# A fused perceiver layer on one core: the order of TensorE's work over the 64 tiles of cross-attention, taken two tiles at a time

## The reference, cut to what matters

```python
x = x + xattn(layernorm(x), ctx)      # x (2,128,128), ctx (2,2048,128), 16 heads of 8
x = x + attn(layernorm(x))            # self-attention over 128 rows, rotary and ALiBi
x = x + ffn(layernorm(x))             # 16 experts of 512, top 4, gelu

# xattn, the part that the change is about
scores = einsum('bhqd,bhkd->bhqk', Qh, Kh) / sqrt(8)
scores = scores - max(scores, axis=-1)
attn = softmax(scores); attn = clip(attn, 1e-12); attn = attn / sum(attn)
ctx = einsum('bhqk,bhkd->bhqd', attn, Vh)
```

## Time and profile before

| | |
|---|---|
| median of 3 runs | 209.88 us (209.35 to 210.08) |
| the profiled execution | 209.72 us, its span 207.8 us |
| TensorE matmul busy | 190.0 us (91%), 2552 instructions |
| VectorE busy | 144.4 us (69%), of it 75.2 us in 64 reductions (L609) |
| ScalarE busy | 143.9 us (69%), of it 69.4 us in 128 exponentials (L1025) |
| GpSimd busy | 82.4 us (40%) |
| granted TensorE clock | 1.00 of full speed from 34 to 128 us |
| tiles | scores of tile 0 start at 34.71 us, those of tile 34 at 81.27, of tile 52 at 107.66 |
| time outside the tiles | the experts run from about 129.7 us to the end |

### The profile page before, as it was taken

The page is one execution under the profiler, slowest core; times in us unless marked ns, Lnnn a source line. Parts: engine busy times, 40 slices in busy tenths (PEclk is TensorE's granted clock), DMA queues, the critical chain, the costliest instruction groups (busy, mean ns, idle before and its releaser), DMA issues.

```text
span 207.8 us, 6327 instructions
## 1 busy us (share of the span) xinstructions
PE 190.0 (91%) x2552; PEld 134.1 (65%) x2552; DVE 144.4 (69%) x259; ACT 143.9 (69%) x321; POOL 82.4 (40%) x117
## 2 busy tenths in 40 slices
PE   4799988999999989989999999999879999999991
PEld 1335235656666545655655666897759998999981
DVE  5289998797979978989999945856884438222220
ACT  4768766888897978876797976778574545456660
POOL 6222979997786987110201001510000005078400
PEclk9999999999999999999999999999999999999999
DMA  5834333366334732367868701400000000000000
GB/s 122 295 140 183 145 93 93 99 221 226 93 93 105 203 106 78 98 209 214 278 222 250 244 19 24 185 0 0 5 0 0 3 0 13 3 0 5 0 0 21
DMA packets 8688, 21.24 MB, mean 102 GB/s; under 512 B 1664, under 2 KB 2784, under 8 KB 8656
## 3 DMA queue, kind: packets, MB, share of 16 engines
q1 hardware_dynamic: 7344, 19.47, 29.3%
q0 software_dynamic: 592, 0.74, 1.6%
q10 hardware_dynamic: 720, 0.59, 0.9%
HBM read 17.52 MB, written 3.28 MB: 100 GB/s over the span
## 4 chain that ended last, share of the span: by engine, by line
PE 61%; DVE 15%; POOL 7%; DMA 6%; issue 4%; ACT 3%; SPq 2%; ACTq 1%; DVEq 0%
PE ps L1516 13%; PE ps L1266 11%; PE ps L1549 10%; PE ps L1247 8%; PE ps L1212 5%; PE ps L1122 3%; DMA wks<-in_wk 3%; DVE sm L712 2%; PE ps L1116 2%; SPq L327 2%; DMA parts_d<-w1s 2%; POOL wr L505 1%; DVE kst L710 1%; DMA kst<-parts_d 1%; PE ps L1409 1%
## 5 line engine op out<-in xcount | busy, mean ns | idle before, releaser
L609 DVE TENSOR_REDUCE mx<-ps 128x2 f32<-128x1024 f32 x64 | 75.2, 1221 | 7.6 <-PE ps L1212 7.5
L1025 ACT ACTIVATE ex<-ps 128x512 f32<-128x512 f32 x128 | 69.4, 594 | 15.0 <-PE ps L1247 12.1
L1266 PE MATMUL ps<-ex,vau 128*9 128x128 f32 x1024 | 39.9, 274 | 0.5 <-ACT oS L1040 0.4
L1516 PE MATMUL ps<-xT,w1s 128*128 128x128 f32 x256 | 34.4, 278 | 0.2
L1516 PEld LDWEIGHTS ps<-xT,w1s 128*128 128x128 f32 x256 | 31.1, 192 | 1.7 <-ACT cT L1051 0.8
L1247 PE MATMUL ps<-qst,kst 64*128 64x128 bf16 x512 | 30.2, 217 | 1.5 <-ACT ex L1025 1.1
L807 DVE SCALAR_TENSOR_TENSOR xs<-ps,wr,xs 128x128 f32<-128x128 f32 x32 | 11.2, 350 | 28.6 <-PE ps L1549 28.3
L1266 PEld LDWEIGHTS ps<-ex,vau 128*9 128x9 f32 x1024 | 22.0, 90 | 13.7 <-ACT ex L1025 9.7
L1247 PEld LDWEIGHTS ps<-qst,kst 64*128 64x128 bf16 x512 | 18.5, 94 | 16.9 <-ACT ex L1025 9.1
L1212 PE MATMUL ps<-kst,qst 64*128 64x512 bf16 x128 | 27.2, 382 | 1.7 <-DMA kst<-parts_d 0.8
L1051 ACT ACTIVATE cT<-ps,b1s 128x128 f32<-128x128 f32 x64 | 18.2, 370 | 13.8 <-PE ps L1516 13.8
(11 more groups left out here) (205 smaller groups left out, 250.4 us busy)
## 6 DMA issues: line engine op xcount, KB each, us to landing
kst<-parts_d SPq DMA_DIRECT2D x84, 64.0 KB
w1s<-in_w SPq DMA_DIRECT2D x8, 512.0 KB, 4.2
kst<-in_w SPq DMA_DIRECT2D x8, 512.0 KB, 4.5
parts_d<-w1s SPq DMA_DIRECT2D x4, 768.0 KB, 3.8
cT<-in_ctxT SPq DMA_DIRECT2D x3, 512.0 KB, 5.0
cT<-in_ctxT SPq DMA_DIRECT2D x2, 256.0 KB, 5.0
picks<-in_pick ACTq DMA_DIRECT2D x1, 384.0 KB, 5.4
qkvs<-in_qkvw POOLq DMA_DIRECT2D x1, 192.0 KB, 3.6
```

Of the source, the lines that this page charges most:

```text
L609: dve.tensor_reduce(out=mx2[:, b, 2 * pair:2 * pair + 2, f], in_=ps[:, bank:bank + 2, :], axis=AX.X, op=ALU.max).then_inc(s["redA"], 1)
L1025: act.activation(ex[:, e % NE, :], ps[:, EBANK["exp", e], :], ACT.Exp, scale=SCALE).then_inc(s["exp"], 1)
L1266: last = pe.matmul(ps[32 * j:32 * j + DK + 1, 7, 128 * hg:128 * hg + 128], vau[:, NK * b + c, GH * hg + j, :], ex[:, (2 * t + j % 2) % NE, ...
L1516: last = pe.matmul(ps[:, SELF[j % 2], 128 * n:128 * n + 128], w1s[:, f0:f0 + 128], xT[:, (b % B) * S:(b % B + 1) * S], start=True, stop=True)
```

## The change

Tiles with units are issued in twos, an even tile `t` and `t + 1`: 25 pairs, from 0 to 51, but for tiles 32 and 33, which stay single, as do those from 52 on. In a pair TensorE does `scores(t)`, a unit, half 0 of `scores(t + 1)`, a unit, half 1, and then `values(t - 1)` and `values(t)` in one run. If `t` has a ring job, that job and the second unit stand between the two tiles, and `scores(t + 1)` is whole. For that all ring jobs have even tiles now: the value pieces move from 3, 11, 19 to 4, 12, 20, and the projection, normalised rows, qkv and q/k turn by one tile. There are 6 exponential buffers, and the exponential of tile `t` waits for `values(t - 3)` where it waited for `values(t - 2)`. The two new buffers hold `picks` and `qr` before the first tile, so ScalarE waits once for GpSimd's last use of `qr`.

```diff
-        picks = sb("picks", [128, 2, 2, 3, 128], bf16)
...
-        qr = sb("qr", [128, B * S])
...
-        NE = 4
+        NE = 6
         ex = sb("ex", [128, NE, 512])
+        early = ex[:, 4:NE, :].rearrange("p a k -> p (a k)")
+        picks = early[:, 0:768].bitcast(bf16).rearrange("p (q h t m) -> p q h t m", q=2, h=2, t=3)
+        qr = early[:, 768:768 + B * S]
...
-        SMALL_AT = {34: "sums", 36: "heads", 39: "proj", 41: "normed", 43: "qkv", 47: "qkT"}
-        VALS_AT = {3: 5, 11: 6, 19: 7}
+        SMALL_AT = {34: "sums", 36: "heads", 40: "proj", 42: "normed", 44: "qkv", 48: "qkT"}
+        VALS_AT = {4: 5, 12: 6, 20: 7}
...
+        def paired(t):
+            return t // 2 != TILES // 4 and t + 8 + LEAD < N_UNITS
...
-                if u == 51:
+                if u == 52:
                     normed(1, [0])
...
-                if t >= 2:
-                    act.wait_ge(s["pv"], t - 1)
+                if t >= NE // 2:
+                    act.wait_ge(s["pv"], t - NE // 2 + 1)
...
+            act.wait_ge(s["qsq"], 1)
...
+            def two_tiles(t):
+
+                scores(t)
+                next_unit(t)
+                if ring_job(t):
+                    job(t)
+                    next_unit(t + 1)
+                    scores(t + 1)
+                else:
+                    scores(t + 1, (0,))
+                    next_unit(t + 1)
+                    scores(t + 1, (1,))
                 if t:
                     values(t - 1)
+                values(t)
+
+            def one_tile(t):
+
+                scores(t)
+                job(t)
+                next_unit(t)
+                self_first(t)
+                values(t - 1)
+
+            for t in range(0, TILES, 2):
+                if paired(t):
+                    two_tiles(t)
+                else:
+                    one_tile(t)
+                    one_tile(t + 1)
```

More of the change, by code:

```diff
@@ L456, in _ @@
             pool.wait_ge(s["qparts"], 1)
-            link(pool.tensor_tensor(qf[:], qr[:], qp[:, 0, :], ALU.add))
+            link(pool.tensor_tensor(qf[:], qr, qp[:, 0, :], ALU.add))
             pool.tensor_tensor(qsq[:], qf[:], qf[:], ALU.mult).then_inc(s["qsq"], 1)
@@ L580, in q_parts @@
                 dve.wait_ge(s["q0"], 1)
-                link(dve.scalar_tensor_tensor(out=qr[:], in0=ps[:, 7, B * S:2 * B * S], scalar=cols[:, 0:1], in1=qp[:, 0, :],
+                link(dve.scalar_tensor_tensor(out=qr, in0=ps[:, 7, B * S:2 * B * S], scalar=cols[:, 0:1], in1=qp[:, 0, :],
                                               op0=ALU.add, op1=ALU.subtract))
-                link(dve.tensor_copy(qp[:, 1, :], qr[:]))
-                dve.tensor_tensor(qp[:, 2, :], qr[:], qp[:, 1, :], ALU.subtract).then_inc(s["qparts"], 1)
+                link(dve.tensor_copy(qp[:, 1, :], qr))
+                dve.tensor_tensor(qp[:, 2, :], qr, qp[:, 1, :], ALU.subtract).then_inc(s["qparts"], 1)
             def norms_max(bank):
@@ L930, in _ @@
             act.dma_start(wqs[:], wq).then_inc(d_wq, 16)
-            act.dma_start(picks[:].rearrange("p q h t m -> p (q h t m)").bitcast(i32), pick_in).then_inc(d_pick, 16)
+            act.dma_start(early[:, 0:768].bitcast(i32), pick_in).then_inc(d_pick, 16)
             act.wait_ge(s["pool"], 1)
@@ L1481, in next_unit, with job @@
                     unit(t + 8 + LEAD)
[L1483 to L1489, removed]
+            def job(t):
                 if turns(t):
@@ L1496, in _ @@
                     vals(VALS_AT[t], EBANK["vals", VALS_AT[t]])
-                if not ring_job(t - 1):
-                    next_unit(t)
-                self_first(t)
+            def two_tiles(t):
[9 more added lines that the diff above has]
+                    scores(t + 1, (1,))
                 if t:
                     values(t - 1)
+                values(t)
[11 more added lines that the diff above has]
+                    one_tile(t + 1)
             values(TILES - 1)
```

## The result

Over 20 runs the changed kernel takes 210.39 us in the median, the kernel before 209.55 us in as many. The ratio is 1.0041, with a 95% interval of 1.0027 to 1.0054: slower by 0.6 to 1.1 us. The forecast was 210.7 us against 209.88, a ratio of 1.004. In some executions of every kernel here the time is some 3 us longer; the medians count them and the ratios leave them out, and the two of which the profile was kept, of e4 and e12, differ from the others by a tile 0 that starts some 3 us late.

The account below looks back on a forecast made before the run. A ring of three score banks between TensorE and ScalarE bounds the tiles. Tiles 0 to 31 give -0.2 us and 34 to 51 +1.1: +0.9 on 209.72 is 210.6, median 210.7 us; range 209.0 to 212.8 us.

Parts of the forecast that it names:

- The loop: Pairs without a job: exponential, half 1 and two values groups close a loop, 2.48 us against 2.32; eight pairs, +1.3 us.
- the pair at 0: Tiles 0 and 1: this pair has only one values group and comes out even.
- The run of two values groups: Behind half 1 in a pair: both groups to the next scores take 1.00 us, saving 0.12 a pair.
- Turns and value pieces: Pairs 6, 14, 22, 30: 2.98 us against 2.85, +0.5; pairs 4, 12, 20: 3.16 against 3.53, -1.1.
- The stall at tile 30: The turn's wait for GpSimd's maximum terms goes, as the value piece no longer delays unit 31's reduction: -0.9 us.
- Tiles 34 to 51: TensorE's loop even, 26.3 us against 26.4; small jobs behind a unit hold VectorE up, +1.1, bounds 0 and 2.
- The sum: Whole kernel: -0.2 us for tiles 0 to 31 and +1.1 for tiles 34 to 51 give +0.9.
- rival 3: Slower by more: the values run saves nothing, +3.0, or small jobs cost their upper bound; 212 to 213.7 us; chance 0.18.
- At nothing: Two more exponential buffers, space shared by `picks` and `qr`, DMA order and tiles from 52 on: no cost.
- Rival 1: VectorE's slack takes up the small jobs, tiles 34 to 51 stay even: 209.7 us, no change; chance 0.17.
- Rival 2: Faster: the values run is outside the loop, only ScalarE's ring binds, 2.15 us a pair: 205.1 us; chance 0.15.

Follow-up runs that it names:

- e4: The kernel before with only the value pieces moved from tiles 3, 11, 19 to 4, 12, 20, single tiles kept; 208.69 us, ratio 0.9965.
- e12: Kernel before with pairs for value pieces alone, single wait, small jobs one tile later, last five constant loads behind tile 30's maximum terms; 206.76 us, ratio 0.9876.
- e1: The changed kernel with a whole scores group waiting once, for the later of its two exponentials; 209.72 us, ratio 1.0012 to the kernel before.
- e6: The changed kernel with the ring job directly behind the scores again, both units behind it; 210.12 us, ratio 1.0024 to the kernel before.
- e9: The kernel before with only the small jobs moved to the change's tiles, in the old order of single tiles; 208.94 us, ratio 0.9981.
- e5: The changed kernel with four exponential buffers in use instead of six; 220.64 us, ratio 1.0522 to the kernel before.

## Why the prediction was right, and where its sum was off

**The loop.** The claim was that a pair closes over exponential, half 1 and two values groups, at 2.48 against 2.32. The loop is there, step by step, at 2.40. The step that was mis-sized is "half 1 needs the bank of that exponential: 0.43 + 0.74": the 0.74 came from whole groups, which wait twice; a half waits once and starts 0.66 after its exponential starts. e1 shows the reason. Eight pairs cost 0.6 us, not 1.3, and the pair at 0, which was put at even, took 2.20, 0.1 less than before. The run of two values groups took 0.99, as the 1.00 that was worked out from the earlier trace rows.

**Turns and value pieces.** 2.98 and 3.17 measured, 2.98 and 3.16 forecast. In a pair with a turn the wait was for a whole group, and 0.74 was right; a pair with a value piece goes by TensorE's own issue.

**The stall at tile 30.** Forecast to go, -0.9. It went, and e4 alone takes 0.92 off these tiles. Its cause, the value piece in front of unit 31, is shown by that.

**Tiles 34 to 51.** Forecast 1.1 more, measured 27.92 - 26.39 = 1.5 more. Both causes named are in the trace: longer waits of VectorE for jobs (0.81 and 0.42 for 0.43 and 0.18), and units that wait for late reductions (0.73 and 0.41 in one pair). e6 gives 0.45 us for the first. What it hid: moving the small jobs is a gain of 0.6 by itself (e9), which I had not seen, so that the pairs' order costs 2.1 on this stretch. I had called TensorE's own loop there even, 26.3 against 26.4; but the 26.4 held the 0.6 that the jobs' old tiles cost, and against e9 a pair's own loop costs 0.7 of the 2.1.

**The sum.** On the tiles the trace has 42.91 - 43.86 + 27.92 - 26.39 = +0.6 us, the forecast had +0.9, the runs give 0.6 to 1.1. Two terms were off in opposite ways, -0.7 and +0.4; so the nearness of the total is partly luck. (Two slips of addition: the terms as written give 210.8 and not 210.7, and rival 3 with the upper bound of the small jobs 211.6 and not 212.)

**At nothing.** The two buffers and the shared space cost nothing that shows. I had not priced the cover: without the buffers the change would have cost 11 us (e5).

**The rivals.** Rival 1 (the small jobs hidden) falls by the 1.5 us. Rival 2 (2.15 a pair) falls: no pair took it, and no values group started before the scores ahead of it. The rule cited against it, from the Trainium skill's page "TensorE: Matmul & The Clock Gate", section "The mechanism", that matmuls start in program order, fits these groups but not all of the trace: at 67.46 a unit's matmul starts ahead of two of half 0 that stand before it (67.50). Where matmuls use only half of the rows, the order in the queue is so not quite the order of the starts. Rival 3's first form (a run that saves nothing) falls by the run's 0.99, against 2 x 0.56 for two groups apart. That agrees with the rule that the prediction cites from the Trainium skill's page "TensorEngine Tiling (Array Packing)", section "Key Properties", that a change of tiling mode drains TensorE; that the 0.12 is the price of the mode is not shown, since the number type changes with it. Its second form, a small-job term at its bound of 2, did not come: against before the stretch lost 1.5, between the forecast and the bound.

## What to carry to other kernels

Before work is grouped to save switches on one engine, follow the loop through the buffers that engines hand to each other, and see which group comes to stand behind its wait: here two value products came behind a wait for a bank and made the loop longer than the switches saved. Test each part of a change alone, since parts can pull apart: moving three jobs by a tile, pairing only the three tiles that have them and dropping a redundant wait give 1.2% together, while pairing all tiles loses 0.4%. And when a fixed chain on another engine feeds the tiles, look whether a gain ahead of it only makes them wait.

## What the runs showed of the hardware that was not expected

Two waits of TensorE on the same counter, the later of which implies the earlier, are not free: one became a semaphore instruction of 51 ns in its queue (60 of them, 23 without), and a late group started 0.09 us earlier without it. Products of one tile shape run on without a gap when they follow one another: 32 value instructions took 0.99 us to the next scores, where two groups of 16 apart took 0.56 each. A group of 4 matmuls on one half of the rows held TensorE as long as 8 on both halves, 0.32 against 0.33 us, so a split in halves is not free. And matmuls on different halves of the rows can start out of their order in the queue, by 0.04 us in the pair above.
